# First attention of a four-layer kernel: scores in eight 32x32 tiles over two PSUM banks, values of a batch's own columns, later loads

## The chip, the cores and the metric

The kernel runs on one core of a Trainium2 chip. The metric is the device time of one execution in microseconds (us). The engines are TensorE (PE in the rows; its weight loads are PEld), VectorE (DVE), ScalarE (ACT), GpSimd (POOL) and the queue of SyncE (SP), which issues most transfers.

## The reference, cut to what matters

The program is four layers of attention and FFN over x of 16 batches, 64 rows and 512 columns. The change touches the first attention alone, a windowed one over the 512 columns of each batch:

```python
HEADS, WINDOW = 8, 16                   # B, C, T = 16, 64, 512; hd = 8
q = Wq x + bq; k = Wk cond + bk; v = Wv cond + bv      # 64 x 64 weights, per column
k, v = pad(k, (8, 7)), pad(v, (8, 7))                  # along T
idx = arange(T)[:, None] + arange(W)[None, :]          # a window of 16 for each column
dots = einsum('bhdt,bhdtw->bhtw', qh, k[:, :, idx]) * hd ** -0.5
attn = softmax(dots, axis=-1)
out = einsum('bhtw,bhdtw->bhdt', attn, v[:, :, idx])
return Wo out + bo
```

Each attention works on a layer norm of x and adds its result to x. The first FFN follows: two int8-like quantisations of a norm of x (gate and up), silu(gate) times up, a third quantisation, and the product with w_down.

## The kernel before

x lies as eight tiles X[:, t, :] of 128 partitions (two batches of 64 rows) and 512 columns. The first attention goes in 32 units u = 4 t + g, each a tile t and a quarter g of its columns (128 columns). A unit's scores are 128 x 512: 128 partitions of head pairs and rows, 16 groups of 32 keys. Stages of a unit stand some steps apart (the list `l0` in stage_order): norm, qk (once a tile), project (values), scores, sum (softmax denominators), turn (transpose of the probabilities), weigh (probabilities times values), out (Wo, added to X). The first FFN of a tile runs between the stages of later units, in the stages f0_*.

One list ORDER, written out by stage_order, gives every engine its order: each engine walks through ORDER and issues what it has for a stage. An engine's instructions run strictly in that order, except for the early weight loads of PE. Steps hand over through semaphores. psum_uses names the bank of each result; psum_table numbers the fillings of each bank in ORDER, and whoever fills a bank waits (p.free, p.n) until every earlier filling of that bank has been given back. A matmul over f32 operands leaves two records in the trace, one over bf16 or fp32r operands one.

What the prediction speaks of, by the lines of the profile:

- L775, L779: queries and keys of a tile (l0_qk), banks 4 and 7. ACT reads the queries at L1774 (frees bank 4).
- L795, L799: values of a unit (l0_project), 16 matmuls of 128 columns into bank 2, and the pad at a tile's edges. wv0 holds the weight of one batch on a half of its rows, zero elsewhere.
- L813, L817: scores (l0_scores). Four matmuls of 512 columns put the window mask, then 32 matmuls of 64 columns add q times k; four 32x32 tiles on the diagonal of the array, all into one bank, 0 or 1 in turn.
- DVE L1372, L1377: row maxima, and their subtraction, which gives the score bank back. ACT L1787 takes exp, DVE L1381 and L1384 the reciprocal sums, POOL L2158 the product.
- L828: transposes of the probabilities (bank 3). L844: weighing, 32 matmuls of 32 columns in eight 64x32 tiles, over banks 4 and 5; ACT L1804 gives them back. L859: output projection (l0_out, bank 6), given back by DVE L1392, which adds it to X.
- L750: transposes of quantised integers: f0_turn (gate, bank 7), f0_turn_u (up, bank 0 for tiles 0 to 5) and f0_turn2. ACT L1836 takes them out as qgT, quT and qiT. ACT L1817 makes the integers.
- L880, L882: gate and up products (f0_gate), read by DVE L1417 and L1418. L896 to L900: f0_down (bank 6), read by DVE L1443.
- DVE L1268, L1272, POOL L2128, L2131 and DVE L1286: layer norm; L1286 waits for POOL's rs.
- SP L2303: every load. In begin it issues all rows of x, the FFN's weights, the transposed context cT (8 loads, in pieces of 256 bytes) and two pieces of the second attention's w1; then cn, the context of tile t + 1, at l0_norm.

Beyond about 211 us the second attention begins (l1_*, L912 and on), and PE is busy nearly throughout.

## Time and profile before

| what | us |
|---|---|
| median of 3 runs | 1567.65 |
| lowest and highest | 1567.29, 1570.88 |
| the profiled execution, its device time | 1568.3 |
| its span (first to last instruction) | 1566.5 |
| busy in it: PE, DVE, ACT, POOL | 1489.1, 819.6, 748.8, 439.2 |

Rows of a timeline give an instruction's start and length, engine, line, operation, output and inputs, how many records in a row it stands for, and in brackets the idle time of the engine before it and what ended that. "issue" there means that the profile shows no releaser. Matmuls overlap in the pipeline, so the distance from one run's start to the next run's start is the time that the run costs; the length of a row reaches further. PEclk is the granted clock of PE as a share of its full speed.

### The profile page before, as it was taken

How to read it: one execution, taken by the hardware profiler on the slowest of the kernel's cores; microseconds unless marked ns; L12 is line 12 of the kernel's file. 1: busy time of each engine (PE TensorE's matmuls, PEld its weight loads, DVE VectorE, ACT ScalarE, POOL GpSimd, SP SyncE). 2: the span in 40 equal slices, each digit the busy share in tenths (PEclk: the TensorE clock that was granted, in tenths of full speed). 3: DMA queues.
4: the chain of work that ended last, by engine and by line, in shares of the span. 5: the costliest groups of instructions: out<-in, count | busy, mean ns of one | idle time of the engine just before them, and what ended most of it. 6: DMA issues, size and time to landing. Idle time of an engine off the chain costs nothing. (4 is left out here: it accounts for less than half of the span.)

```text
span 1566.5 us, 32999 instructions
## 1 busy us (share of the span) xinstructions
PE 1489.1 (95%) x13154; PEld 1228.5 (78%) x13154; DVE 819.6 (52%) x1681; ACT 748.8 (48%) x2560; POOL 439.2 (28%) x557
## 2 busy tenths in 40 slices
PE   6988979999999999999999999879999999999998
PEld 4767768888989888888989887556656778888876
DVE  3678875544444555544443447766665421343465
ACT  4565545454545445454544565355443312455552
POOL 1355343222222212222222224255221000123333
PEclk8999999999999999999999999899999999999999
DMA  8000010020100101010010110020100001122111
GB/s 252 13 17 10 10 44 28 28 75 28 41 28 3 40 27 41 28 41 28 4 38 28 41 55 1 2 83 1 41 1 1 26 6 56 48 74 74 47 27 62
DMA packets 44537, 58.62 MB, mean 37 GB/s; under 512 B 25520, under 2 KB 32704, under 8 KB 41568
## 3 DMA queue, kind: packets, MB, share of 16 engines
q1 hardware_dynamic: 43872, 56.05, 11.4%
q8 instruction: 104, 1.70, 0.5%
q10 hardware_dynamic: 448, 0.46, 0.1%
q14 instruction: 49, 0.40, 0.1%
q0 software_dynamic: 64, 0.00, 0.0%
HBM read 48.89 MB, written 2.10 MB: 33 GB/s over the span
## 5 line engine op out<-in xcount | busy, mean ns | idle before, releaser
L1872 ACT ACTIVATE big<-pb 128x128 f32<-128x128 f32 x384 | 106.5, 277 | 300.9 <-PE pb L912 198.2
L2211 POOL TENSOR_TENSOR big<-big 128x512 f32<-128x512 f32 x96 | 99.9, 1040 | 260.4 <-DVE big L1503 260.4
L1921 ACT ACTIVATE big<-pb,big 128x128 f32<-128x128 f32 x384 | 135.7, 367 | 58.0 <-issue 34.2
L1498 DVE TENSOR_REDUCE big<-pb 128x4 f32<-128x512 f32 x96 | 65.8, 686 | 178.1 <-PE pb L951 170.5
L927 PE MATMUL pb<-wkh,CXh 128*128 128x256 f32 x512 | 150.0, 293 | 0.0
L927 PE MATMUL pb<-wkl,CXh 128*128 128x256 f32 x512 | 145.4, 284 | 0.0
L927 PE MATMUL pb<-wkh,CXl 128*128 128x256 f32 x512 | 144.6, 282 | 0.0
L2201 POOL TENSOR_SCALAR big<-big 128x6 f32<-128x6 f32 x64 | 12.8, 199 | 413.1 <-ACT big L1872 412.5
L1290 DVE TENSOR_TENSOR X<-X,pb 128x512 f32<-128x512 f32 x128 | 86.9, 679 | 74.8 <-PE pb L1138 39.3
L978 PE MATMUL pb<-woh,oh 128*128 128x512 f32 x256 | 114.3, 446 | 0.0
L912 PE MATMUL pb<-wqh,CXh 128*128 128x512 f32 x256 | 101.9, 398 | 3.0 <-DVE big L1468 1.5
L978 PE MATMUL pb<-woh,ol 128*128 128x512 f32 x256 | 103.1, 403 | 0.0
L978 PE MATMUL pb<-wol,oh 128*128 128x512 f32 x256 | 102.0, 399 | 0.0
L912 PE MATMUL pb<-wqh,CXl 128*128 128x512 f32 x256 | 101.3, 396 | 0.0
L912 PE MATMUL pb<-wql,CXh 128*128 128x512 f32 x256 | 101.2, 395 | 0.0
L966 PE MATMUL pb<-big 128*128 128x256 f32 (+1 forms) x384 | 98.8, 380 | 0.1
L927 PEld LDWEIGHTS pb<-wkh,CXl 128*128 128x128 f32 x512 | 97.8, 191 | 0.0
L927 PEld LDWEIGHTS pb<-wkh,CXh 128*128 128x128 f32 x512 | 97.5, 190 | 0.0
L927 PEld LDWEIGHTS pb<-wkl,CXh 128*128 128x128 f32 x512 | 97.4, 190 | 0.0
L1488 DVE COPY big<-pb 128x512 f32<-128x512 f32 x56 | 38.7, 690 | 101.5 <-PE pb L939 101.0
L2128 POOL TENSOR_SCALAR ve<-mv 128x1 f32<-128x1 f32 x64 | 14.3, 224 | 274.7 <-DVE mv L1272 272.6
L2206 POOL TENSOR_TENSOR big<-big,half 128x6 f32<-128x6 f32 x64 | 84.7, 1324 | 9.4
(279 smaller groups left out, 3790.7 us busy)
## 6 DMA issues: line engine op xcount, KB each, us to landing
big<-in_w SPq DMA_DIRECT2D x17, 1024.0 KB, 5.0
big<-in_w SPq DMA_DIRECT2D x24, 256.0 KB, 3.0
big<-in_w SPq DMA_DIRECT2D x8, 512.0 KB, 3.6
o<-o SPq DMA_DIRECT2D x96, 32.0 KB, 1.9
X<-in_x SPq DMA_DIRECT2D x8, 256.0 KB, 5.4
big<-in_cn SPq DMA_DIRECT2D x8, 256.0 KB, 2.8
CXlf<-in_cT SPq DMA_DIRECT2D x8, 256.0 KB, 5.9
big<-in_wa SPq DMA_DIRECT2D x1, 2048.0 KB, 7.6
```

Source lines behind the costliest of these rows:

```text
L912: a = pe.matmul(bank(p), x_rows(x, c, t), y[:, 512 * c:512 * c + 512], start=(n == 0), stop=(n == 11))
L927: a = pe.matmul(bank(p)[:, s * 256:s * 256 + 256], kv_rows(x, c, 2 * t + s), y[:, 256 * c:256 * c + 256], start=(n == 0), stop=(n == 11), ...
L966: a = pe.matmul(bank(p)[0:hd, s * 256:s * 256 + 256], v_of(s), pt[:, s * 256:s * 256 + 256], start=(s == 0), stop=True, skip_group_check=True)
L978: a = pe.matmul(bank(p), x[:, 128 * c:128 * c + 128], y[:, 512 * c:512 * c + 512], start=(n == 0), stop=(n == 3 * size - 1))
L1290: v.tensor_tensor(X[:, t, :], X[:, t, :], bank(p), ADD).then_inc(p.free, 1)
L1488: v.tensor_copy(QT[i % 2].rearrange("p (b h q) -> p h b q", b=2, h=4), bank(p).rearrange("p (h b q) -> p h b q", h=4, b=2)).then_inc(p.fre ...
L1498: v.tensor_reduce(m[j % 2], quarters(bank(p)), AX, MAX, negate=True).then_inc(S.m, 1)
L1872: y = a.activation(sq[i % 2], bank(p)[:, j * width:j * width + 128], ACT.Square, accum_out=ss[i % 2][:, first + j:first + j + 1])
L1921: y = a.activation(e_[:, c], bank(p)[:, c], ACT.Exp, bias=m[j % 2][:, k:k + 1], scale=1.0, accum_out=z[j % 2][:, k:k + 1])
L2128: g.tensor_scalar(ve[:, n % 4, :], mv[:, n % 4, 1:2], 1e-5, None, ADD).then_inc(*on.to(S.pool))
L2206: g.tensor_tensor(rr[i % 2][:, 0:6], ss[i % 2][:, 0:6], half[:, 0:6], ALU.pow).then_inc(*on.to(S.rr))
L2211: g.tensor_tensor(quarters(e_), quarters(e_), bc(r[j % 2], 128), MUL).then_inc(*on.to(S.pn))
```

## The change

Scores go in eight 32x32 tiles: the four on the diagonal as before write 256 columns (keys of the quarter's first four groups) into bank 0, and four more, which take the same rows but write partitions shifted by 64, write the other 256 columns into bank 1. The mask is put by eight matmuls of 256 columns instead of four of 512. One unit now fills both banks at once, so psum_uses books bank 1 for each unit, and nothing else may use bank 0 at that time: f0_turn_u of tiles 0 to 5 moves to bank 6, and l1_q(0) waits for the last scores to be read. Each value projection writes only the 64 columns of its own batch (in pieces of 16) into bank 2, whose other columns DVE zeroes once at the start; the host's column order and masks (`order`, `pairs`, `own`) change with it, as does the column picked in the weighing. SP issues the cT loads at l0_norm of unit 4 and the w1 loads at that of unit 8.

```diff
--- before.py
+++ after.py
@@ -240,7 +240,7 @@
     if stage == "l0_project":
         return [("v", (2,))]
     if stage == "l0_scores":
-        return [("S", (0, 1))]
+        return [("S", (1,))]
     if stage == "l0_turn":
         return [("T", (3,))]
     if stage == "l0_weigh":
@@ -250,7 +250,7 @@
     if stage == "f0_turn":
         return [("g", (7 if i < NT - 2 else 5 if i < NT - 1 else 4,))]
     if stage == "f0_turn_u":
-        return [("u", (0 if i < NT - 2 else 3 if i < NT - 1 else 6,))]
+        return [("u", (6 if i < NT - 2 else 3 if i < NT - 1 else 6,))]
     if stage == "f0_turn2":
         return [("p", (3,))]
     if stage in ("f0_down", "l1_turn") and i == NT - 1:
@@ -452,6 +452,8 @@
         def bank(use):
             return banks[use.bank // 2][:, 512 * (use.bank % 2):512 * (use.bank % 2) + 512]
 
+        two_banks = banks[0].rearrange("p (e n) -> p e n", e=2)
+
         X = sb("X", [128, NT, 512])
         ident = sb("ident", [128, 128])
         identb = sb("identb", [128, 128], BF16)
@@ -787,13 +789,15 @@
                 on.wait_ge(d_cn, n_cn)
                 on.wait_ge(S.zero, 2)
                 on.wait_ge(p.free, p.n)
+                on.wait_ge(S.zero, 9)
                 for k in range(4):
                     for r in range(2):
                         for b in range(2):
                             key, at = slice(64 * r + 32 * b, 64 * r + 32 * b + 32), g * 128 + k * 32 + r * 16
                             rows_ = slice(64 * b, 64 * b + 64)
-                            a = pe.matmul(bank(p)[key, k * 128:k * 128 + 128], cn[rows_, at:at + 32], wv0[rows_],
-                                          start=(k == 0), stop=True, skip_group_check=True)
+                            a = pe.matmul(view(bank(p)[key], k * 128 + 16 * b, [[32, 4], [1, 16]]), cn[rows_, at:at + 32],
+                                          view(wv0[rows_], 16 * b, [[32, 4], [1, 16]]), start=(k == 0), stop=True,
+                                          skip_group_check=True)
 
                 if g in (0, 3):
                     a = pe.matmul(bank(p)[:, g * 128:g * 128 + 128], pad[0:16, g // 3 * 128:g // 3 * 128 + 128],
@@ -802,19 +806,22 @@
 
             def l0_scores(u):
                 t, g = divmod(u, 4)
-                p, q, k = PSUM["l0_scores", u, "S"], PSUM["l0_qk", 4 * t, "q"], PSUM["l0_qk", 4 * t, "k"]
+                q, k = PSUM["l0_qk", 4 * t, "q"], PSUM["l0_qk", 4 * t, "k"]
+                p = PSUM["l0_scores", u, "S"]
                 on.wait_ge(q.free, q.n + 1)
                 on.wait_ge(k.free, k.n + 1)
                 on.wait_ge(S.band, 4)
                 on.wait_ge(p.free, p.n)
-                pairs = [slice(32 * h, 32 * h + 32) for h in range(4)]
-                for r in pairs:
+
+                tiles = [(e, slice(32 * h, 32 * h + 32), slice((32 * h + 64 * e) % 128, (32 * h + 64 * e) % 128 + 32))
+                         for e in range(2) for h in range(4)]
+                for e, r, c in tiles:
                     b = bandb[r.start:r.start + 16]
-                    pe.matmul(bank(p)[r], b[:, 0:32], b[:, 128:640], start=True, stop=False, skip_group_check=True)
-                for i in range(8):
-                    n = 8 * g + i
-                    for r in pairs:
-                        a = pe.matmul(bank(p)[r, i * 64:i * 64 + 64], Qx[t % 2][r, n * 32:n * 32 + 32],
+                    pe.matmul(two_banks[c, e, 0:256], b[:, 0:32], b[:, 128:384], start=True, stop=False, skip_group_check=True)
+                for i in range(4):
+                    for e, r, c in tiles:
+                        n = 8 * g + 4 * e + i
+                        a = pe.matmul(two_banks[c, e, i * 64:i * 64 + 64], Qx[t % 2][r, n * 32:n * 32 + 32],
                                       view(K0[t % 2][r], n * 16, [[560, 2], [1, 32]]), start=False,
                                       stop=True, skip_group_check=True)
                 a.then_inc(p.full, 1)
@@ -840,7 +847,7 @@
                 for j in range(4):
                     for p, r in zip((p0, p1), halves):
                         for h in range(4):
-                            c = j * 128 + 32 * h
+                            c = j * 128 + 32 * ((h + j // 2 * 2) % 4)
                             a = pe.matmul(bank(p)[32 * h:32 * h + 32, j * 32:j * 32 + 32],
                                           VW[u % 4][r, j * 128 + 32 * h:j * 128 + 32 * h + 32], PT0[u % 2][r, c:c + 32],
                                           start=(j == 0), stop=True, skip_group_check=True)
@@ -904,6 +911,9 @@
                 h, t = divmod(i, NT)
                 p = PSUM["l1_q", i, "p"]
                 lt_ready("l1", t)
+                if i == 0:
+                    scores = PSUM["l0_scores", 4 * NT - 1, "S"]
+                    on.wait_ge(scores.free, scores.n + 1)
                 on.wait_ge(p.free, p.n)
                 n = 0
                 for c in range(4):
@@ -992,7 +1002,7 @@
                 n = weight_turn(i)
                 if n is not None:
                     on.wait_ge(S.mx4, n + 1)
-                    on.wait_ge(S.zero, 9)
+                    on.wait_ge(S.zero, 10)
                     turn_b(PSUM["l1_d", i, "w4"], q4[n % 2])
                 k = slice(512 * (i % 2), 512 * (i % 2) + 512)
                 project(PSUM["l1_d", i, "p"], PSUM["l1_v", i, "p"], 4, (oh[:, k], ol[:, k], woh, wol), S.wol,
@@ -1349,6 +1359,7 @@
                         v.memset(view(Kbd[k], edge, [[560, 2], [1, 8]]), 0.0).then_inc(S.zero, 1)
                 v.memset(mg, -MAGIC).then_inc(S.zero, 1)
                 v.memset(mgp, MAGIC).then_inc(S.zero, 1)
+                v.memset(bank(PSUM["l0_project", 0, "v"]), 0.0).then_inc(S.zero, 1)
 
             def l0_bias(_):
                 on.wait_ge(D.ident, 16)
@@ -1367,14 +1378,16 @@
 
             def l0_scores(u):
                 p = PSUM["l0_scores", u, "S"]
-                s3, p3 = [x.rearrange("p (g k) -> p g k", k=32) for x in (em[u % 3], bank(p))]
+                s4 = em[u % 3].rearrange("p (e g k) -> p e g k", e=2, k=32)
+                p4 = two_banks[:, :, 0:256].rearrange("p e (g k) -> p e g k", k=32)
+                m3 = mx0[u % 2].rearrange("p (e g) -> p e g", e=2)
                 on.wait_ge(p.full, p.n + 1)
-                on.mark(v.tensor_reduce(mx0[u % 2], p3, AX, MAX))
+                on.mark(v.tensor_reduce(m3, p4, AX, MAX))
                 if u >= 3:
                     turned = PSUM["l0_turn", u - 3, "T"]
                     on.wait_ge(turned.full, turned.n + 1)
                 on.wait_ge(S.dve, on.n)
-                v.tensor_tensor(s3, p3, bc(mx0[u % 2], 32), SUB).then_inc(p.free, 1)
+                v.tensor_tensor(s4, p4, m3.unsqueeze(3).broadcast_to([128, 2, 8, 32]), SUB).then_inc(p.free, 1)
 
             def l0_sum(u):
                 on.wait_ge(S.exp0, u + 1)
@@ -2324,11 +2337,6 @@
                 for dst, name in ((wgu[0], "wg"), (wgu[1], "wu"), (wd, "wd"), (ig, "ig"), (iu, "iu"), (ii, "ii"), (sgw, "sgw"),
                                   (suw, "suw"), (sdw, "sdw")):
                     load(dst, d[name], D.f0)
-                for c in range(4):
-                    for k in range(2):
-                        load(view(cT, c * 2048 + 192 * k, [[256, 8], [1, 64]]), d["cT"][:, c, k], D.ct)
-                load(wq1, d["w1"][0][:, 0:2048], D.wq1)
-                load(w1, d["w1"][0][:, 2048:3072], D.kv1)
 
             def l0_norm(u):
                 t = u // 4
@@ -2339,6 +2347,13 @@
                 on.wait_ge(v.full, v.n + 1)
                 on.wait_ge(k.full, k.n + 1)
                 load_cn(t + 1)
+                if t == 1:
+                    for c in range(4):
+                        for k in range(2):
+                            load(view(cT, c * 2048 + 192 * k, [[256, 8], [1, 64]]), d["cT"][:, c, k], D.ct)
+                if t == 2:
+                    load(wq1, d["w1"][0][:, 0:2048], D.wq1)
+                    load(w1, d["w1"][0][:, 2048:3072], D.kv1)
 
             def l1_begin(_):
                 on.wait_ge(S.wql, 4)
@@ -2504,11 +2519,11 @@
         z[64:, 64:] = w
         return z
 
-    order = np.arange(128).reshape(2, 8, 8).transpose(1, 0, 2).reshape(128)
+    order = np.arange(128).reshape(2, 4, 16).transpose(1, 0, 2).reshape(128)
     p = np.arange(128)
     bq, bk, bv, bo = [np.tile(i[f"L0_xattn_b{n}"], 2)[:, None] for n in "qkvo"]
-    pairs = (p[:, None] // 16 % 2 == np.arange(2)[None, :]).astype(np.float32)
-    own = (p[:, None] // 8 % 2 == np.arange(2)[None, :]).astype(np.float32)
+    pairs = (p[:, None] // 8 % 2 == np.arange(2)[None, :]).astype(np.float32)
+    own = (p[:, None] // 16 % 2 == np.arange(2)[None, :]).astype(np.float32)
     m["w0"] = np.concatenate([diag(i["L0_xattn_Wq"].T)[:, order], diag(i["L0_xattn_Wk"].T)[:, order],
                               diag(i["L0_xattn_Wv"].T)[:, order], np.where(pairs > 0, bq[order], 0), np.where(own > 0, bk[order], 0), pairs, own], 1)
     m["wo0"] = np.concatenate([diag(i["L0_xattn_Wo"].T)[order], bv[order], pairs, bo], 1)
```

On PE, around the second gate transposes of a tile (L750 before, L752 after), with the buffer numbers and waits. pb0 holds banks 0 and 1, pb1 banks 2 and 3, pb2 4 and 5, pb3 6 and 7. Before:

```order
L859 MATMUL pb3<-big 128x128 [waits bank6_free,bank5_free,bank4_free]
L859 MATMUL pb3<-big 128x128
L844 MATMUL pb2<-big 32x32 [waits bank3_free]
L844 MATMUL pb2<-big 32x32 x31
L750 MATMUL pb0<-ident,big 128x128 [waits bank0_free,f0_q_up]
L750 MATMUL pb0<-ident,big 128x128 x3
L828 MATMUL pb1<-ident,big 128x128 [waits l0_probs]
L828 MATMUL pb1<-ident,big 128x128 x3
L880 MATMUL pb3<-CXh,qgT 128x256 [waits bank7_free,f0_low]
L882 MATMUL pb3<-wgl,qgT 128x256
```

After:

```order
L866 MATMUL pb3<-big 128x128 [waits bank6_free,bank5_free,bank4_free]
L866 MATMUL pb3<-big 128x128
L851 MATMUL pb2<-big 32x32 [waits bank3_free]
L851 MATMUL pb2<-big 32x32 x31
L752 MATMUL pb3<-ident,big 128x128 [waits bank6_free,f0_q_up]
L752 MATMUL pb3<-ident,big 128x128 x3
L835 MATMUL pb1<-ident,big 128x128 [waits l0_probs]
L835 MATMUL pb1<-ident,big 128x128 x3
L887 MATMUL pb3<-CXh,qgT 128x256 [waits bank7_free,f0_low]
L889 MATMUL pb3<-wgl,qgT 128x256
```

The rows stand in the same order; f0_turn_u writes bank 6 and waits for bank6_free, of which the last filling before it is that of L866, four rows up.

On the SP queue, from the load of suw on. Before:

```order
L2303 DMA big<-in_suw 128x256
L2303 DMA big<-in_sdw 128x512
L2303 DMA CXlf<-in_cT 128x8x64 x8
L2303 DMA big<-in_w 128x2048
L2303 DMA big<-in_w 128x1024
L2303 DMA big<-in_cn 128x512 [waits bank7_full,bank2_full] x6
```

After:

```order
L2316 DMA big<-in_suw 128x256
L2316 DMA big<-in_sdw 128x512
L2316 DMA big<-in_cn 128x512 [waits bank7_full,bank2_full]
L2316 DMA CXlf<-in_cT 128x8x64 x8
L2316 DMA big<-in_cn 128x512 [waits bank7_full,bank2_full]
L2316 DMA big<-in_w 128x2048
L2316 DMA big<-in_w 128x1024
L2316 DMA big<-in_cn 128x512 [waits bank7_full,bank2_full] x4
```

The loads of cT stand behind the first waiting load of cn, the first two loads of w1 behind the second one.

## Rows read from the trace of the kernel before

**Rows 1.** The page: busy time of the engines, and the instruction queue of TensorE.

```profile
PE 1489.1 (95%) x13154; PEld 1228.5 (78%) x13154; DVE 819.6 (52%) x1681; ACT 748.8 (48%) x2560; POOL 439.2 (28%) x557
...
q8 instruction: 104, 1.70, 0.5%
```

**Rows 2.** Windows: stretch, length, then busy us (records) of each engine, PEclk, DMA.

```profile
112.02:123.33 11.31, 11.06 (x381) 9.00 (x382) 8.20 (x19) 5.52 (x12) 7.83 (x10) 1.00 0.02 5
...
75.41:101.93 26.52, 24.17 (x730) 19.26 (x727) 21.03 (x46) 16.14 (x34) 13.41 (x16) 1.00 0.05 14
101.93:130.61 28.68, 25.05 (x734) 19.57 (x733) 22.03 (x47) 17.30 (x36) 16.18 (x19) 1.00 0.04 12
```

**Rows 3.** Timeline of PE, 101 to 131: start, length, instructions, [idle before <-releaser].

```profile
102.26 0.40 PE L813 MATMUL pb<-big 16*32 16x512 bf16 x4
102.49 1.06 PE L817 MATMUL pb<-big 32*32 32x64 f32 x64
103.48 1.08 PE L795 MATMUL pb<-big 64*32 64x128 f32 x32
104.49 0.48 PE L799 MATMUL pb<-big 16*128 16x128 f32 x2
...
108.04 0.92 PE L844 MATMUL pb<-big 64*32 64x32 f32 x64 [0.71 <-issue]
...
112.03 1.06 PE L795 MATMUL pb<-big 64*32 64x128 f32 x28 [0.93 <-issue]
...
119.53 0.76 PE L844 MATMUL pb<-big 64*32 64x32 f32 x64
120.22 0.66 PE L828 MATMUL pb<-ident,big 128*128 128x128 f32 x4
120.80 0.39 PE L813 MATMUL pb<-big 16*32 16x512 bf16 x4
...
123.34 0.27 PE L795 MATMUL pb<-big 64*32 64x128 f32 x1 [0.24 <-issue]
...
125.68 0.66 PE L750 MATMUL pb<-ident,big 128*128 128x128 f32 x4 [0.35 <-ACT big L1817]
126.17 0.60 PE L828 MATMUL pb<-ident,big 128*128 128x128 f32 x4
127.94 0.38 PE L880 MATMUL pb<-CXh,qgT 128*128 128x256 f32 x1 [1.17 <-ACT qgT L1836]
```

**Rows 4.** Timeline of DVE, 101 to 131.

```profile
116.77 0.75 DVE L1443 SCALAR_TENSOR_TENSOR big<-pb,big 128x512 f32<-128x512 f32 x1 [1.18 <-PE pb L900]
...
119.13 0.69 DVE L1377 TENSOR_TENSOR big<-pb,big 128x512 f32<-128x512 f32 x1
...
128.04 0.55 DVE L1286 TENSOR_SCALAR xn<-X,mv,rs 128x512 f32<-128x512 f32 x1 [0.99 <-POOL rs L2131]
128.50 0.35 DVE L1392 SCALAR_TENSOR_TENSOR X<-pb,big,X 128x128 f32<-128x128 f32 x1
...
130.61 0.48 DVE L1417 SCALAR_TENSOR_TENSOR big<-pb,big 128x256 f32<-128x256 f32 x1 [0.88 <-PE pb L882]
```

**Rows 5.** Timeline of DVE, at the first and at the last of the six gates.

```profile
72.91 0.34 DVE L1392 SCALAR_TENSOR_TENSOR X<-pb,big,X 128x128 f32<-128x128 f32 x1
...
75.41 0.48 DVE L1417 SCALAR_TENSOR_TENSOR big<-pb,big 128x256 f32<-128x256 f32 x1 [1.27 <-PE pb L882]
...
209.95 0.35 DVE L1392 SCALAR_TENSOR_TENSOR X<-pb,big,X 128x128 f32<-128x128 f32 x1
...
211.44 0.48 DVE L1417 SCALAR_TENSOR_TENSOR big<-pb,big 128x256 f32<-128x256 f32 x1 [0.26 <-PE pb L882]
```

**Rows 6.** Timelines of PE and of the SP queue, first 35 us.

```profile
33.92 0.52 PE L817 MATMUL pb<-big 32*32 32x64 f32 x9 [3.18 <-issue]
...
16.26 14.83 SPq L2303 DMA_DIRECT2D CXlf<-in_cT  x8
```

## The prediction

> **What bounds the kernel now.** I read three things, in this order. The page's first section says that TensorE (PE) is busy 95% of the span, with 13154 matmul and 13154 weight-load records [rows 1]. The change touches only the first attention, which runs beside the first FFN until about 211 us; so I cut that stretch into tiles, from one start of DVE L1417 (the first read of a finished gate product) to the next, and asked for busy times [rows 2]. In the tile 101.93 to 130.61 PE is busy 25.05 of 28.68 us, DVE 22.03, ACT 17.30, POOL 16.18. PE is not alone: PE and DVE hand the period to each other. The engine timelines of that tile [rows 3, 4] show where.
>
> In a tile's first half DVE waits for PE: before L1443 it stands 1.18 us until the last L900. In its second half, L1443 at 116.77 to L1392 at 128.50, DVE has 11.7 us of work in fixed order, with one visible wait of 0.99 us for POOL's rs; PE is ahead there, transposes quantised rows (L750 at 125.68), and then stands 1.17 us before the gate matmuls (L880) until ACT has qgT. DVE closes the tile 1.8 us after its last L1392 (end 128.85, L1417 at 130.61).
>
> There is a third limit, PE's instruction supply. 26308 PE instructions came in 104 instruction packets [rows 1]: 253 each. In dense stretches PE stops in the middle of a run that waits for no semaphore: 0.93 us before the last 28 of 32 L795 at 112.03, 0.24 us before the last one at 123.34 [rows 3]. Between these two places stand 381 + 382 = 763 instructions, three times 254, in 11.31 us [rows 2]: 3.8 us for each packet's worth. A mid-run stop is PE waiting for its next packet.
>
> **PE work per unit (32 units).** From start to start [rows 3]: four band matmuls of 512 columns take 0.23 us (L813 to L817), the 32 score matmuls of 64 columns 0.99 us (64 records, to L795), 16 value projections of 128 columns 1.01 us (32 records, to L799). The weighing, 64 records of 32 columns in eight tiles, takes 0.69 us (119.53 to 120.22).
> Half the columns, half the time: 15.5 ns a record at 64 columns, 31.6 at 128, with four tiles in flight in both. So a record of 64 columns holds its tile for about 62 ns. Scores in eight tiles would need 7.8 ns a record, but the closest records I see in such a stream are 10.8 ns apart (0.69/64), so I take 64 x 10.8 = 0.69 us; bounds 0.69 and 0.99. Projections at 64 columns have the shape of today's scores: 32 x 15.5 = 0.50 us; bounds 0.35 (32 x 10.8) and 1.01. Eight band matmuls of 256 columns: between half of 0.23 and 0.23, taken 0.15. Sum: 0.08 + 0.30 + 0.51 = 0.89 us less PE work a unit, 28 us over 32 units, if nothing else held.
>
> Can eight tiles overlap when they share four groups of rows? The weighing shows it: a record of 32 columns holds its tile for 31 ns, they start every 10.8 ns, so 2.9 are in flight on only two groups of rows. The Trainium skill ("TensorE: Matmul & The Clock Gate", Part 3) says that a weight load overlaps running matmuls only where the row group differs, which speaks against this edit; by that rule scores would stay at 0.99 us and the saving would be 0.59 us a unit. The weighing row contradicts it.
>
> **What of this reaches the end: supply.** The change adds four band matmuls a unit, 8 instructions, 256 in all: one packet more. It makes dense stretches denser. From the weighing at 108.04 to the end of L900 stand about 500 instructions, two packets. PE did them in 8.7 us, 0.93 of it stopped; with 0.89 us less work (one score and one projection run) it would meet a packet not yet there once or twice. At 3.5 to 3.8 us a packet, most of the saving turns into such stops. The start of that stretch does not move: L844 at 108.04 stands 0.71 us although L859 is done, because it needs bank 4 back from ACT's reading of the queries, which comes behind DVE's scores subtraction and exp. So per tile the gain lies between 0 and 1.8 us (0.89 + 0.93); I take 0.4, the lower side because the supply rows are the nearest. Five tiles: -2.0 (0 to -9).
>
> **The bank move.** f0_turn_u (L750, second of the pair) for tiles 0 to 5 goes from bank 0 to bank 6. Bank 6 also holds l0_out, issued by PE just before (L859), and is given back by DVE's L1392. The order listing shows the wait change from bank0_free to bank6_free. Today L750 starts at 125.68, and that L1392 ends at 128.85, because DVE is nearly a step behind. After the change PE stands there until 128.9, and behind it in PE's queue wait the transposes L828 and the whole gate (L880, L882). Then: L750 0.49 us (to 126.17), L828 0.4 to 0.5, gate to L1417 2.67 at most (127.94 to 130.61, with short waits in it) and 2.2 without: 3.1 to 3.7 us from the end of L1392 to L1417, taken 3.2. Today these six distances are 2.2, 1.8, 1.8, 1.3, 1.3 and 1.1 us, 9.4 together (first, third and last in [rows 4, 5]). Six tiles: 19.2 - 9.4 = **+9.8** (9.2 to 12.8). Nothing hides it: DVE has only L1381 and L1384 (0.9 us) to do meanwhile. What held the gate before, ACT's qgT, is ready in time and no longer late.
>
> **One score buffer instead of two.** Scores u+1 now wait for DVE's L1377 of u. The tightest place: L1377 from 119.13, 0.69 us long, against the next L813 at 120.80 [rows 3, 4]: 1.0 us of slack, of which PE's saving of one projection run takes 0.5. Cost 0, bounds 0 and 0.5 a tile where DVE is late.
>
> **Zeroing a bank.** One DVE memset of 128x512, about the 0.69 us of L1377, before the first x row has landed, where DVE has nothing else to do. Cost 0. The values' pad and weights are only reordered.
>
> **Later loads.** The eight cT loads keep the SP queue busy for 14.83 us from 16.26 [rows 6]. They now go behind the third cn load, when the fourth projection is done (about 24 us), and the two w1 loads behind the fourth cn load, near 48 us. Their first user, ACT's split of the context, comes tens of us later: no cost there. But packets of instructions wait behind bulk loads: PE stopped 3.18 us at 33.92, mid-run [rows 6], far more than the 0.93 of a quiet stretch. In the gap around 22 to 24 us one packet comes sooner, worth 1 to 2 us with the PE savings; then cT covers about 24 to 40 instead of 16 to 31, which hits one or two packets again; the w1 loads fall beside a wait for queries near 53 us. I take -1.5 for everything before 75 us (-4 to +4).
>
> **Sum.** Profiled execution 1568.3 us: 1568.3 - 2.0 + 9.8 - 1.5 = 1574.6. That execution lies 0.65 us over the median of 1567.65, so the forecast is 1573.9. From 211 us on DVE and ACT hand the work on one by one, so a late sixth gate moves the end by all of it.
>
> **Rivals.**
> B, the supply does not bind: chance 0.25. For: most runs of the tile shown have no stop in them. Against: 0.93 at 112.03. Each tile then gains 1.4 (0.89 and half of 0.93): -7 + 9.8 - 1.5 = +1.3, 1569.0. The Trainium skill ("Runtime: NRT & Kernel Launch", Instruction fetch mechanics) holds that crossing a 16 KiB block is mostly hidden. The rows at 112.03 and 123.34 disagree.
> C, faster: the bank wait is short because PE's saved time is what lets DVE's L1392 come earlier than the transposes. It decides if L1392 comes before L750 is ready; then six tiles lose nothing and gain 1.4 to 1.8 with the first 75 us gaining 3: 1567.65 - 9 - 3 = 1556 to 1562. Against: L1392 is 11.7 us of DVE work behind L1443. Chance 0.10.
> D, slower still: cT and w1 now meet a PE that needs packets, two more of them coming 3 us late (3.18 at 33.92): 1573.9 + 6 = 1580. Chance 0.10.
> E, the change does not do what it says: eight tiles run as four, scores stay at 0.99 us and the added band matmuls cost 0.1 a unit: +1.5 on mine, 1575. Chance 0.05.
> Mine: 0.50, its own range 1569 to 1578.
>
> **Numbers.** A measurement of this kernel tells about 0.3%, 4.7 us. Slower than 1572.4: three quarters of mine, D, E: 0.52. Faster than 1562.9: C and a little of B: 0.11. Between: 0.37. The range 1563.5 to 1579.5 leaves out C and half of D.
>
> **What the profile after will show.** L750 of f0_turn_u idle 2 to 4 us with DVE L1392 as releaser, and L1417 3.2 us behind L1392's end. Score run to the next 0.69 us, projection 0.50 us. Mid-run stops of PE, a packet apart, more often. Tiles 27 to 29.5 us where [rows 2] has 26.5 and 28.7. No idle before L813 that ends with L1377, except early. It is wrong if L750 is not idle, or if the tiles' DVE waits before L1443 vanish whole.

## The result, and the profile after

The changed kernel takes 1590.89 us (median of 4 runs, 1586.27 to 1595.95), the kernel before beside it 1567.47 (1563.49 to 1570.88). The ratio is 1.0151 with the interval [1.0111, 1.0191]: **slower by 23.4 us**, where +6.2 was forecast. The direction was right and so was the place of the largest loss; the size was not, and the time lies above the range. The profiled execution is the fastest of the four, so its trace shows less of the loss than the medians do. The profiled execution took 1586.27 us, 18.0 over that of before.

The page of the changed kernel: from its section on busy time, on the 40 slices (tenths) and on the DMA queues.

```profile
PE 1474.9 (93%) x13282; PEld 1220.7 (77%) x13282; DVE 820.1 (52%) x1682; ACT 750.4 (47%) x2560; POOL 440.0 (28%) x557
...
PE   5887777899999999999999999779999999999998
...
PEclk7789999999999999999999999999999999999999
...
q8 instruction: 105, 1.72, 0.4%
```

Against [rows 1] PE has 128 records more, one instruction packet more, and 14 us less busy time. It also is granted less clock: the first three slices read 7, 7 and 8, where the page of before has 8, 9 and 9. The windows from gate to gate (starts of the first gate read, L1417 before and L1430 here) answer [rows 2]. Columns: window, its length, busy time and records of each engine, PEclk, DMA share, GB/s.

```profile
0.00:81.33 81.33, 58.30 (x1704) 43.92 (x1712) 36.86 (x86) 38.33 (x75) 18.50 (x29) 0.75 0.42 127
81.33:110.41 29.08, 22.67 (x746) 18.58 (x741) 20.94 (x47) 16.37 (x34) 14.95 (x17) 0.87 0.05 13
110.41:140.90 30.49, 22.95 (x750) 18.87 (x749) 21.90 (x47) 17.27 (x36) 16.24 (x18) 0.89 0.04 12
140.90:170.44 29.54, 22.84 (x750) 18.66 (x749) 21.36 (x47) 15.75 (x33) 12.63 (x15) 0.95 0.04 12
```

The tile that took 28.68 us now takes 30.49, and the one before it 29.08 instead of 26.52. In the first of these PE is busy 2 us less, at a mean clock of 0.89 where it was 1.00. The first gate comes 5.9 us later (81.33 against 75.41), the sixth 21.9 us later (233.36 against 211.44), the eighth 20.3 (310.86 against 290.53). From the eighth gate to the end of the span the kernels take 1276.0 and 1273.6 us: most of what is late at the gates is late at the end (21.9 us at the sixth gate, 18.0 at the end; the prediction had all of it).

Two rows of the waits between 60 and 250 us (who waited <- for whom: us in total, times, longest) name the spot.

```profile
DVE big L1430 <- PE pb L889: 24.5, 6, 4.7
...
PE pb L752 <- DVE X L1405: 19.7, 6, 4.4
```

L752 is the transpose of f0_turn_u ("the turn" from here on) and L1405 the output addition that gives bank 6 back (L750 and L1392 before). The expectations below call it the down products' addition in some places; the rows show the output addition. "The gate" is the run of sixteen gate and up products, L887 and L889. Before, no wait of L750 for L1392 is among the wait rows. The PE timeline of one such place (start, busy time, line, tile, records, then the idle time ahead and its releaser):

```profile
101.86 0.35 PE L851 MATMUL pb<-big 64*32 64x32 f32 x31 [0.21 <-issue]
105.84 1.08 PE L752 MATMUL pb<-ident,big 128*128 128x128 f32 x4 [3.62 <-DVE X L1405]
106.72 1.06 PE L835 MATMUL pb<-ident,big 128*128 128x128 f32 x4
107.43 0.56 PE L887 MATMUL pb<-CXh,qgT 128*128 128x256 f32 x1
107.79 0.41 PE L889 MATMUL pb<-wgl,qgT 128*128 128x256 f32 x1
...
109.27 0.28 PE L887 MATMUL pb<-CXl,quT 128*128 128x256 f32 x1
109.38 0.28 PE L889 MATMUL pb<-wul,quT 128*128 128x256 f32 x1
```

Windows of the same place: while PE waits, the first 2.2 us after, and the last gate products.

```profile
102.30:105.80 3.50, 0.00 (x0) 0.00 (x0) 2.39 (x6) 2.71 (x7) 1.45 (x3) 0.51 0.00 0
105.84:108.00 2.16, 2.16 (x10) 2.16 (x11) 0.70 (x2) 0.88 (x2) 1.20 (x2) 0.50 0.03 8
109.27:110.20 0.93, 0.93 (x10) 0.93 (x9) 0.00 (x0) 0.00 (x0) 0.00 (x0) 1.00 0.00 0
```

PE has stood 3.62 us when bank 6 comes free, and goes on at a granted clock of 0.50, the lower of its two levels (1.2 GHz). From the turn's start to the next run's start pass 0.88 us where [rows 3] has 0.49, and a gate product is 0.41 us long instead of 0.28. At 109.27 the clock is back at 2.4 GHz, but eight of the sixteen gate products are done by then. DVE's timeline shows who pays.

```profile
105.35 0.35 DVE L1405 SCALAR_TENSOR_TENSOR X<-pb,big,X 128x128 f32<-128x128 f32 x1
105.61 0.68 DVE L1394 TENSOR_REDUCE big<-big 128x16 f32<-128x512 f32 x1
106.32 0.26 DVE L1397 RECIPROCAL big<-big 128x16 f32<-128x16 f32 x1
110.41 0.48 DVE L1430 SCALAR_TENSOR_TENSOR big<-pb,big 128x256 f32<-128x256 f32 x1 [3.83 <-PE pb L889]
```

From the end of L1405 (105.70) to L1430 pass 4.7 us; I call this distance **the gap**, since the prediction's sum is made of it. The six gaps of tiles 0 to 5 are 5.5, 4.7, 4.9, 4.5, 5.5 and 4.7 us, 29.8 in all. They were 9.4 before; the prediction had 19.2. The idle time in front of these six turns is 1.7, 3.6, 3.9, 2.6, 3.6 and 4.4 us, and the clock fell behind, or during, every one.

### The profile page after: what moved, and what is told of

Same layout as the page of the kernel before. It is cut to its first block and busy times, and to the rows that moved or that the text cites. A ratio compares the mean times of both kernels' runs of the same rounds, so it can differ in the third digit from the quotient of the medians.

```text
span 1584.5 us, 33248 instructions
## 1 busy us (share of the span) xinstructions
PE 1474.9 (93%) x13282; PEld 1220.7 (77%) x13282; DVE 820.1 (52%) x1682; ACT 750.4 (47%) x2560; POOL 440.0 (28%) x557
```

## The experiments

Times are medians; "over before" is against the runs of the kernel before on the same chip (medians of 1567.1 to 1567.5). "Half clock" is the time ahead of 300 us that PE's granted clock was at its lower level in the profiled execution: 20.5 us before, 75.1 after. It is one execution of each kernel, and it varies: the kernels "after" and "after, wait filled" are the same program until the first moved turn, and the mean granted clock of their first 71 us is 0.76 and 0.83. The ratio in the table is not always that of the two medians; where that matters the text says so.

| kernel | us | ratio [interval] | six gaps, us | half clock, us |
|---|---|---|---|---|
| before | 1567.5 | | 9.4 | 20.5 |
| after | 1590.9 | 1.0151 [1.0111, 1.0191] | 29.8 | 75.1 |
| bank move alone | 1582.4 | 1.0110 [1.0086, 1.0135] | 30.0 | 44.4 |
| bank move, wait filled | 1576.5 | 1.0057 [1.0040, 1.0073] | 19.9 | 17.1 |
| after, wait filled | 1582.7 | 1.0101 [1.0084, 1.0118] | 19.7 | 44.4 |
| after, output products first | 1575.6 | 1.0053 [1.0033, 1.0072] | 20.9 | 47.8 |
| before, output products first | 1567.8 | 1.0005 [0.9991, 1.0019] | 17.3 | 17.1 |
| scores and bank move | 1588.3 | 1.0129 [1.0109, 1.0150] | 28.1 | 61.4 |
| scores, turn in bank 2 | 1570.4 | 1.0019 [0.9999, 1.0039] | 13.6 | 47.8 |
| the same, output products first | 1569.6 | 1.0018 [1.0006, 1.0031] | 20.2 | 30.7 |
| own-column values alone | 1568.6 | 1.0009 [0.9995, 1.0023] | 8.8 | 30.7 |
| the same, output products first | 1568.8 | 1.0007 [0.9995, 1.0019] | 18.1 | 44.4 |
| late loads alone | 1568.6 | 1.0008 [0.9994, 1.0021] | 8.8 | 27.3 |
| after with early loads | 1591.9 | 1.0158 [1.0140, 1.0177] | 31.3 | 88.7 |
| one score buffer alone | 1566.8 | 1.0005 [0.9991, 1.0019] | 9.0 | 20.5 |
| scores and bank move, padded | 1592.1 | 1.0144 [1.0104, 1.0183] | 26.0 | 51.2 |
| after, padded | 1589.4 | 1.0137 [1.0106, 1.0168] | 24.7 | 58.0 |

### Each edit by itself

The bank move alone:

```diff
-        return [("u", (0 if i < NT - 2 else 3 if i < NT - 1 else 6,))]
+        return [("u", (6 if i < NT - 2 else 3 if i < NT - 1 else 6,))]
```

> The kernel before with f0_turn_u of tiles 0 to 5 in bank 6, nothing else. Theory (the bank wait, then half clock behind it, costs the time): the end of DVE's L1392 to L1417 grows from 1.2 to 2.2 us to 4.5 to 5.5 us at each of six gates, granted clock falls behind each, +15 to +22 us. Rival (single score buffer or later loads cost the time, the bank wait is hidden in DVE's lag): under +6 us.

1582.4, +14.9, at the low edge of what was expected (the ratio, 1.0110, makes it +17): this one line is about two thirds of the loss. Its waits between 60 and 250 us, and PE's timeline at one gate, with all of PE's work as before:

```profile
DVE big L1417 <- PE pb L882: 24.7, 6, 4.7
...
PE pb L750 <- DVE X L1392: 19.6, 6, 4.6
```

```profile
133.14 0.83 PE L750 MATMUL pb<-ident,big 128*128 128x128 f32 x4 [3.06 <-DVE X L1392]
133.77 1.06 PE L828 MATMUL pb<-ident,big 128*128 128x128 f32 x4
134.48 0.56 PE L880 MATMUL pb<-CXh,qgT 128*128 128x256 f32 x1
134.84 0.41 PE L882 MATMUL pb<-wgl,qgT 128*128 128x256 f32 x1
```

The same wait, the same slow products behind it. The other edits alone:

```diff
-        return [("S", (0, 1))]
+        return [("S", (1,))]
```

> The kernel before with the scores of every unit in bank 1 instead of banks 0 and 1 in turn, bank 0 left to f0_turn_u as it is. Theory (1 us of slack or more at the tightest place): PE does not wait for DVE's L1377 outside the first 60 us, 0 to +3 us. Rival (single buffering is the main loss): +8 us or more, with idle before L813 that ends with L1377.

1566.8, no difference to be told from none.

```diff
-                for c in range(4):
-                    for k in range(2):
-                        load(view(cT, ...), d["cT"][:, c, k], D.ct)
-                load(wq1, ...)
-                load(w1, ...)
...
                 load_cn(t + 1)
+                if t == 1: ...   # the cT loads
+                if t == 2: ...   # wq1, w1
```

> The kernel before with the cT and w1 loads issued at l0_norm of units 4 and 8, nothing else. Theory: the first gate's L1417 comes 0 to 3 us later than 75.4 us, total +1 to +4 us. Rival (loads cost most of the loss, packets of instructions wait behind them): +8 us or more.

1568.6, +1.0, which isn't to be told from none either. The reverse, the changed kernel with these loads back in their early place:

> The changed kernel with its loads put back where the kernel before has them. Theory one, late loads are free here as they were alone (+1.1 us, not told from none): 1588 to 1593 us, first gate at about 81 us, six gates behind the down products near 29 us in all. Theory two, the loads' place and the spared work act together through the clock (the tensor engine idles early): 1582 to 1587 us, the first gate at 76 to 79 us and less half clock ahead of 70 us.

1591.9 against 1590.9: its first gate does come earlier (79.57 against 81.33), though not as early as the second theory had it, but the half clock does not shrink (88.7 us) and the time is the same. No part of the 23 us can be told as the loads'.

```diff
-                            a = pe.matmul(bank(p)[key, k * 128:k * 128 + 128], cn[rows_, at:at + 32], wv0[rows_],
+                            a = pe.matmul(view(bank(p)[key], k * 128 + 16 * b, [[32, 4], [1, 16]]), cn[rows_, at:at + 32],
+                                          view(wv0[rows_], 16 * b, [[32, 4], [1, 16]]),
```

(with the zeroed bank and the host's orders that belong to it)

> The kernel before with value projections of a batch's own 64 columns into the zeroed bank and the host's column order that goes with it, scores and banks as before. Theory: 0.43 us less PE work a unit, part of it lost to instruction supply and to DVE: -2 to -7 us. Rival (strided pieces of 16 columns or the supply eat it all): within 1.5 us of the kernel before.

1568.6: no gain, a miss. In every unit the projection run is 0.4 us shorter, 13 us over 32 units, and nothing of it arrives.

### Is it the clock behind the wait?

The first test of this puts work into the wait. PE does 24 transposes into bank 3 ahead of each moved turn, work that nothing uses:

```diff
             def f0_turn_u(t):
                 on.wait_ge(S.qu, t + 1)
+                if t < NT - 2:
+                    ...                      # bank 3 of the next l0_turn is free
+                    for c in range(24):
+                        pe.transpose(bank(T)[:, 0:128], xu0[:, 0:128], ident[:, :])
                 turn_ints(PSUM["f0_turn_u", t, "u"], xu0, 4)
```

> The changed kernel with 24 transposes more before each of the six f0_turn_u, into bank 3, which is free there; their output is overwritten and used by nothing. They take 24 x 0.122 = 2.9 us of PE while it would wait for bank 6. Theory (the wait of about 3.5 us is paid once itself and a second time as half clock behind it): clock stays full behind the six, L1405's end to L1430 falls from 4.5 to 5.5 us to 3.1 to 3.7 us, and the kernel gains 6 to 12 us on the changed one, though PE has more to do. Rival (the 4.5 to 5.5 us come from the order of ACT and the gate's own inputs): no gain or slower by the added work.

1582.7: 8.2 us faster than the changed kernel although it has 144 transposes more. Then the same with the bank move and nothing else:

> The bank move alone (1582.4 us) with 24 transposes ahead of each of the six moved turns, so that the tensor engine works where it would wait for bank 6; nothing uses what they write. This isolates the failed step: at full clock that step's sum was +9.8 us on the kernel before. If half clock behind the wait is what the sum lacked: gaps of 3.0 to 3.3 us six times (19 us in all) behind the down products' addition instead of 30.0, and 1574 to 1579 us, 4 to 8 below the bank move alone, although 144 instructions are added. If the clock is a bystander: the gaps stay near 5 us and the time is 1582 to 1586.

1576.5, inside what was expected, +9.4 over before. PE's timeline at one gate, DVE's beside it, and the window of that tile:

```profile
127.06 2.84 PE L874 MATMUL pb<-ident,big 128*128 128x128 f32 x24 [0.53 <-ACT big L1823]
130.28 0.66 PE L750 MATMUL pb<-ident,big 128*128 128x128 f32 x4 [0.38 <-DVE X L1398]
130.78 0.60 PE L828 MATMUL pb<-ident,big 128*128 128x128 f32 x4
131.14 0.37 PE L886 MATMUL pb<-CXh,qgT 128*128 128x256 f32 x1
131.34 0.28 PE L888 MATMUL pb<-wgl,qgT 128*128 128x256 f32 x1
```

```profile
129.88 0.34 DVE L1398 SCALAR_TENSOR_TENSOR X<-pb,big,X 128x128 f32<-128x128 f32 x1
...
133.31 0.48 DVE L1423 SCALAR_TENSOR_TENSOR big<-pb,big 128x256 f32<-128x256 f32 x1 [2.20 <-PE pb L888]
```

```profile
104.41:133.31 28.90, 26.83 (x758) 21.92 (x757) 22.08 (x47) 17.16 (x36) 16.23 (x19) 1.00 0.04 13
```

The bank still comes free only when DVE's addition ends (L1398 in this kernel), so the wait is there, but PE spends it at work, the clock stays at 1.00, and the gap is 3.1 us. Five of the six gaps lie between 3.06 and 3.08; the first is 4.5, since there the filler lasts longer than the wait and itself holds the turn up. The prediction's term, 3.2 us each and +9.8 in all, is what this kernel measures: +9.4 (6.3 to 11.4 by the interval). The clock is the rest of the bank move: 5.9 us by the medians, 8.3 by the ratios.

### Taking the wait away instead

Output products ahead of the rows of the norm in the list of the first attention's steps, so that DVE's addition comes earlier against the turn:

```diff
-l0 = [("l0_rows", 1), ("l0_out", 7), ...
+l0 = [("l0_out", 7), ("l0_rows", 1), ...
```

> The changed kernel with l0_out ahead of l0_rows in each step, so that DVE runs L1405 before it stands for POOL's rs and before the norm of a new tile. Theory: L1405 comes 1.4 us earlier at each gate, PE's wait falls from 3.3 to about 1.9 us, short enough that the clock keeps up; 8 to 18 us less than the changed kernel. Rival (DVE is the bound, the order inside a step moves nothing): within 3 us of it.

1575.6, 15.3 us less than the changed kernel: two thirds of the loss gone with nothing of the change undone. PE at one of its gates:

```profile
122.94 0.30 PE L851 MATMUL pb<-big 64*32 64x32 f32 x17 [0.43 <-issue]
124.93 0.63 PE L752 MATMUL pb<-ident,big 128*128 128x128 f32 x4 [1.70 <-DVE X L1405]
```

Behind this wait of 1.70 us the four transposes take 0.63 us, at full clock; behind 3.62 us they took 1.08. (At the last of the six gates this kernel still waits 5.46 us and falls to half clock.) The length of one wait doesn't decide it alone. The changed kernel's first gate has the same 1.70 us, and a mid-run stop shortly before it as well (0.75 us; 0.43 above):

```profile
73.61 0.63 PE L851 MATMUL pb<-big 64*32 64x32 f32 x49 [0.75 <-issue]
75.94 1.09 PE L752 MATMUL pb<-ident,big 128*128 128x128 f32 x4 [1.70 <-DVE X L1405]
```

There the transposes take 1.09 us and the whole gate behind them runs at 0.50. The other way round, the kernel with scores and bank move waits 2.22 us before its fourth turn (163.06), 0.69 us of stop shortly before, and stays at full clock. The same order in the kernel before:

> The kernel before with the output products put ahead of the normalised rows in the list of the first attention's steps, as in the run that took 15.3 us off the changed kernel. If that order helps by itself, the gap from the down products' addition to the gate shrinks from 9.4 us in all and the time falls to 1560 to 1565 us. If it helps only where the turned products wait for the down products, nothing is there to be had: 1566 to 1569 us, which I expect after the run with the values edit and this order (1568.8).

1567.8, nothing: there the turn does not wait for that addition. (Its gaps sum to 17.3 us and cost nothing, so with this order a gap is no longer a loss: DVE's addition simply comes earlier. Gaps compare kernels of one order only.) With the values edit alone:

> The kernel before with own-column values and l0_out ahead of l0_rows. Theory: DVE fills its 0.99 us stand for POOL with L1392, which ends 1 us earlier in each tile; with PE's 0.43 us a unit: -3 to -9 us against the kernel before. Rival (the supply of instructions bounds the dense stretches): within 2 us of it.

1568.8, a miss of the expected 3 to 9 us.

### What the spared work is worth

Eight-tile scores with the turned products in bank 2, which the values leave early, so that the wait for bank 6 is out:

```diff
-        return [("u", (0 if i < NT - 2 else 3 if i < NT - 1 else 6,))]
+        return [("u", (2 if i < NT - 2 else 3 if i < NT - 1 else 6,))]
```

> The kernel before with scores in eight tiles over banks 0 and 1, and f0_turn_u of tiles 0 to 5 in bank 2 behind ACT's copy of the values, not bank 6; values whole, loads early. The wait is then for ACT L1761, 1.6 us instead of 3.2 us. Theory: the clock stays full after it and 0.3 us less PE work a unit comes back: -3 to +4 us against the kernel before. Rival (eight tiles in one group of rows each do not overlap, or the single buffer holds PE up): +6 us or more, with a score run of 0.99 us.

1570.4: +2.9 over before, within what was expected, with gaps 4.2 us longer in all than before. With the output products first:

> The run with eight-tile scores and the turned products in bank 2 (1570.4 us, gaps from the down products' addition to the gate 13.6 us in all), with the output products put first. If the order takes the wait for bank 2 away as it took that for bank 6: gaps 9 to 10 us in all, 1563 to 1568 us, which would be a version as fast as the kernel before or a little faster. If the spared work turns into stops and half clock anyway: 1568 to 1572 us, with half-clock time ahead of 300 us at 40 us or more.

1569.6: the time of the second of the two cases, though its trace has 30.7 us of half clock and not the 40 or more that went with it. No version that keeps part of the change is faster than the kernel before clear of noise. Now the scores edit on top of the bank move:

> The kernel before with two of the change's edits, the eight-tile scores and the bank move (which needs the single buffer). The bank move alone gave 1582.4 us, the whole change 1590.9. My theory for the 8.5 us between them: work that the tensor engine is spared beside the moved bank turns into stops and idle time and then into half clock (1.2 GHz), so that the scores edit on top of the bank move costs time: 1585 to 1590 us, six gates behind the down products 3 to 5.5 us each (27 to 32 us in all), and more half-clock time ahead of 300 us than the 44.4 us of the bank move alone. Rival, that the edits add: the scores edit with the turned products in bank 2 gave 1570.4 (+3 on before), so 1582 to 1585.5 and about 45 to 55 us of half clock. Rival, that what is missing lies in the loads or the values: within 1.5 us of 1582.4.

1588.3: by the medians 5.9 us more than the bank move alone, as the first theory had it, though PE has less to do. By the ratios it is 3 us, and the two intervals overlap, so this step alone is not clear of noise. With the values edit on top it is: the changed kernel with early loads is the bank move plus scores plus values, and its interval (from 1.0140) lies above that of the bank move alone (to 1.0135), 9.5 us apart by the medians. PE's work and clock in the windows of 0 to 80 and 80 to 300 us, of the bank move alone:

```profile
0.00:80.00 80.00, 61.89 (x1762) 46.59 (x1763) 39.94 (x90) 39.82 (x79) 18.54 (x29) 0.94 0.44 130
80.00:300.00 220.00, 184.37 (x4307) 155.44 (x4306) 147.69 (x319) 111.90 (x281) 89.47 (x105) 0.92 0.06 19
```

and with the scores:

```profile
0.00:80.00 80.00, 59.00 (x1803) 43.64 (x1804) 38.82 (x89) 38.99 (x77) 18.47 (x29) 0.89 0.43 129
80.00:300.00 220.00, 180.28 (x4367) 150.27 (x4366) 146.12 (x315) 111.74 (x281) 88.21 (x104) 0.90 0.06 19
```

PE is busy less in both, at a lower clock in both. That isn't the luck of one trace: the mean granted clock over the span, on record for every execution, is 0.980 to 0.983 in the four of the bank move alone and 0.974 to 0.977 in the four with the scores. The values edit alone shows the same, a mean of 0.985 over ten executions against 0.989 over the 25 of the kernel before beside it, and so do the mid-run stops: between 60 and 240 us those above 0.2 us sum to 1.2 us in the trace of the bank move alone and to 6.0 with the scores. If less work brings the half clock, then putting work back should cost nothing; the mask products of one bank were written once more in each of the 32 units, and the real ones write over them:

```diff
+                for e, r, c in tiles[4:]:
+                    b = bandb[r.start:r.start + 16]
+                    pe.matmul(two_banks[c, e], b[:, 0:32], b[:, 128:640], start=True, stop=False, ...)
                 for e, r, c in tiles:
```

> The bank move and the eight-tile scores (1588.3 us), with the four 512-column mask products of one bank done once more ahead of each of the 32 score units; the real mask products write over them. It adds 128 instructions and, by the kernel before's 0.23 us for four such, 7.4 us of work, two thirds of what the scores edit saved. My theory, that work saved where the stream is dense comes back as stops and half clock: the padded kernel is no slower, 1583 to 1589 us, with less half-clock time ahead of 300 us than 61 us and a fifth tile's wait nearer 13.4 than 18.5 us. Rival, work is work: 1592 to 1596 us.

> The changed kernel (1590.9 us) with the same padding, 7.4 us of work that the mask products' second writing adds. By the theory that spared work comes back as stops and half clock: 1585 to 1592 us, half-clock time ahead of 300 us below 75 us. By work is work: 1595 to 1599 us.

1592.1 and 1589.4: +3.8 and -1.5 against the kernels without it. The first is the rival's number, the second lies inside the theory's bounds, and neither difference is clear of noise. The padding was also smaller than the expectations made it: it runs beside the real mask products, the score block takes 1.04 us from start to start instead of 0.89, and so it adds 4.8 us in all and not 7.4. The half clock shrank in both profiled executions (61.4 to 51.2 us, 75.1 to 58.0). These two runs settle nothing: +3.8 is near the padding's size, -1.5 is not, and whether the spared work itself makes the loss stays open.

## Why the prediction missed

Two steps failed. By the medians the forecast was 17.0 us short, 5.1 of it in the first step and the rest in the second.

**The size of the bank-move term, +9.8.** Its mechanism stood: the turn idles with the addition as releaser, six times, with the transposes and the whole gate queued behind it, and nothing hides it. Its working took the turn, L828 and the gate at full-clock rows, 3.2 us a gap. Behind these waits they ran at 1.2 GHz for most of the time and the gap was 4.5 to 5.5 us. With the clock held up by filler the term measures +9.4; without, +14.9. (The six gaps grew by 20.6 us in the trace of the bank move alone, the sixth gate came 18.5 late and the end 15.2: gaps show where the loss is and overstate it.)

**The terms for spared work and for everything before 75 us, -2.0 and -1.5.** They came out at +8.5 together, the changed kernel over the bank move alone (about 6.5 by the ratios). The prediction let the supply take back most of the saving, but never more than all of it, and it never asked about the clock. The runs show that spared work gives nothing back (four kernels with less work for PE and without the move to bank 6: +1.0 to +2.9 us) and that the granted clock falls with it. How that makes a loss of this size stays open.

The trace of before held the row for the first step. In the early stretch PE stops 3.18 us mid-run [rows 6], and the windows around that stop (up to it, behind it, and after) read:

```profile
29.05:33.92 4.87, 1.69 (x63) 1.27 (x63) 0.00 (x0) 1.83 (x6) 0.78 (x1) 0.99 0.74 159
33.92:40.70 6.78, 6.78 (x135) 5.02 (x139) 3.79 (x7) 3.27 (x7) 0.00 (x0) 0.51 0.77 274
40.70:45.00 4.30, 4.25 (x188) 3.42 (x184) 1.58 (x3) 1.84 (x4) 1.05 (x1) 1.00 0.03 8
```

A stop of 3.18 us, and then 6.78 us of work at 0.51. The prediction used this stop as a price for supply and did not ask what the clock did behind it, although it forecast six waits nearly as long. [rows 2] showed 1.00 everywhere because in these tiles PE never stood longer than 1.17 us at once. The Trainium skill says as much ("TensorE: Matmul & The Clock Gate", HAM oscillation — how this bites in real kernels): matmul stretches that are separated by a wait each start at the lower clock; it tells this of waits for DMA. This case's rows agree, at 105.84 and at 33.92, but not for every wait, as the one of 2.22 us above shows.

**PE work per unit.** The predicted 0.15, 0.69 and 0.50 us for masks, scores and projections measure 0.12, 0.76 and 0.58, start to start:

```profile
117.79 0.30 PE L820 MATMUL pb<-big 16*32 16x256 bf16 x8
117.91 0.84 PE L824 MATMUL pb<-big 32*32 32x64 f32 x64
118.67 0.65 PE L798 MATMUL pb<-big 64*32 64x64 f32 x32
119.25 0.48 PE L803 MATMUL pb<-big 16*128 16x128 f32 x2
```

Saved: 0.77 us a unit, 0.89 predicted. Eight tiles do run as more than four (rival E is out): 11.9 ns a record against 15.5.

**Supply.** Rival B's number is out: four kernels with less PE work gained nothing. That fits a supply that binds, but also the clock and DVE's fixed order, and no run parts them. The forecast stops are there, a packet apart and more often: between 60 and 240 us those above 0.2 us are 7 before, 3.6 us in all, and 13 after, 9.9 us. They come at multiples of one distance: one before the last 31 records of L851 at 101.86, another inside a score run:

```profile
128.22 0.65 PE L824 MATMUL pb<-big 32*32 32x64 f32 x40 [0.60 <-issue]
```

```profile
101.86:128.22 26.36, 19.88 (x636) 16.39 (x636) 18.25 (x38) 14.94 (x31) 12.82 (x15) 0.87 0.05 13
```

Between them stand 1272 instructions by the records, five times 254. In the two profiled executions the term of -2.0 for five tiles was about right or a little too good: from the first to the sixth gate the changed kernel takes 16.0 us longer (152.03 against 136.03), its five gaps there 17.0, so the rest of these tiles gained 1.0.

**Everything before 75 us** was given -1.5. The first gate came 5.9 us late; 3.4 of it is its own gap (5.5 against 2.2), 2.5 the stretch ahead, at a mean clock of 0.75 over the first 81 us where before has 0.93 over 75. But the 2.5 is no larger than what two executions differ by: the output addition ahead of the first gate starts at 75.44 in the changed kernel and at 72.47 in the one with filler, the same program up to the turn behind it, against 72.91 before. So the trace doesn't fix the size of this term. The late loads, which the prediction made responsible for either sign, cost nothing that can be told. With the scores edit the clock in that stretch is lower (0.94 to 0.89 in the two pairs of windows above).

**One score buffer, zeroing, extra mask products, later loads**: each at about nothing, as said. Rival C fell at once, since the addition comes 1.7 to 4.4 us after PE is ready for the turn. Rival D's sign was right and its cause wrong.

**In medians** the loss is +9.4 for the wait, +5.5 for the clock behind it, +5.9 for the scores edit on top, and +2.6 for values and loads together. The first two are clear of noise; of the last two only the sum is (the spreads of the kernels are 1581.2 to 1587.5, 1586.1 to 1590.5 and 1586.3 to 1596.0). What of it is lower clock and what is stops stays open.

## What to carry to other kernels

Price a wait that a change adds to TensorE at the wait plus what stands behind it at half clock as the upper bound; look in the trace for any stop of about that length and read the granted clock after it. Where such a wait can't be taken out by order, harmless work inside it was worth 6 to 8 us here. And before sharing a PSUM bank with another user, ask who gives it back and how far behind that engine is, since one bank number cost 14.9 us here, and the shorter matmul runs gave nothing back. Then try each edit of a change by itself, since the one that was to save time may be the one that adds to the loss.

## What was not expected of the hardware

- Behind idle time of 3.1 us or more ahead of a short burst came 1.2 GHz for most of that burst, at every such turn of the changed kernel and of the bank move alone. Shorter idle time went either way: 1.70 us was followed by 0.50 in one place and by 1.00 in another. 24 back-to-back transposes in place of the idle time (2.84 us) kept the clock at 1.00, so transposes alone were enough to keep it up.
- Less work didn't mean less time: projections 0.4 us shorter in each of 32 units moved the time by +1.0 us (interval -0.8 to +3.6), with a mean granted clock of 0.985 instead of 0.989.
- Eight 32x32 tiles over two banks gave 11.9 ns a record of 64 columns, not half of the 15.5 ns that four tiles give.
